# Attention with ternary gate on one core: maxima shared out by VectorE's time, masked keys computed one quad earlier, value transposes placed behind the next product, two groups of loads moved

## What is computed

```python
xn = layernorm(x)                                  # 1e-5
q, k, v = (xn @ W).reshape(B, T, 16, 32)           # for Wq, Wk, Wv
scores = einsum('bthd,bshd->bhts', q, k) * tril(ones((T, T)))
attn = softmax(scores / T ** 0.5)                  # masked keys keep score 0, not -inf
s = einsum('bhts,bshd->bthd', attn, v).reshape(B, T, 512) @ Wo
gate = silu(layernorm(xn, gamma, beta) @ ternary(weight).T + bias)
out = x + s * gate
```

## Time and profile before

| | |
|---|---|
| runs | 1616.06, 1619.94, 1622.37 us; median 1619.94 |
| profiled execution | 1617.84 us, span 1616.1 us, mean granted TensorE clock 0.972 |
| TensorE busy | 1524.8 us, 94% of the span |
| VectorE, ScalarE, GpSimd busy | 1052.3, 775.7, 868.5 us |
| phase A, its end, attention, phase D (us of the span) | 0 to 387, 387 to 420, 420 to 1490, 1490 to 1616 |

### The profile page before, as it was taken

How to read it: one execution, slowest core, us unless ns; L and a number is a source line. 1 busy time by engine, 2 the same in 40 slices (tenths; PEclk the granted TensorE clock), 3 DMA queues, 4 the chain that set the end, 5 groups by cost and what they waited for, 6 DMA issues and landing times.

```text
span 1616.1 us, 24521 instructions
## 1 busy us (share of the span) xinstructions
PE 1524.8 (94%) x8554; PEld 907.5 (56%) x8554; DVE 1052.3 (65%) x2389; ACT 775.7 (48%) x1614; POOL 868.5 (54%) x723
## 2 busy tenths in 40 slices
PE   6999999998799999999999999999999999899886
PEld 5777877786444455455544544544544554343665
DVE  7544765643687767767767776777766777650656
ACT  4333322233345565655656555665565655466110
POOL 4100000000565777877768777777776877469341
PEclk9999999999799999999999999999999999899999
DMA  6658765546931350351154146045025311211998
GB/s 202 188 179 216 237 196 183 157 157 181 215 90 34 80 145 21 82 113 56 35 114 116 35 86 145 15 98 132 23 53 119 92 35 38 89 32 55 305 343 294
DMA packets 110426, 201.42 MB, mean 125 GB/s; under 512 B 14688, under 2 KB 32736, under 8 KB 109280
## 3 DMA queue, kind: packets, MB, share of 16 engines
q1 hardware_dynamic: 99216, 177.86, 40.7%
q10 hardware_dynamic: 11088, 22.02, 4.1%
HBM read 123.22 MB, written 76.28 MB: 123 GB/s over the span
## 4 chain that ended last, share of the span: by engine, by line
PE 76%; DMA 9%; DVE 9%; SPq 2%; issue 1%; ACT 1%; POOL 1%; ACTq 0%; POOLq 0%; DVEq 0%
PE psP L1246 19%; PE psS L1316 17%; PE psO L1339 15%; PE psM L1224 14%; PE psL L1345 6%; DMA half<-mrow 3%; DMA gr<-gate 3%; DVE psM L1038 3%; DVE mx L1041 2%; PE psL L1354 2%; PE psT L1171 2%; DMA half<-k_lo 1%; SPq L546 1%; DMA rb<-r_rows 1%; ACT Pb L904 1%
## 5 line engine op out<-in xcount | busy, mean ns | idle before, releaser
L784 POOL TENSOR_TENSOR acc<-acc,Pb 128x1024 f32<-128x1024 f32 (+2 forms) x308 | 598.0, 1971 | 181.9 <-PE psO L1339 142.1
L904 ACT ACTIVATE Pb<-psS 128x512 f32<-128x512 f32 (+2 forms) x1122 | 519.6, 533 | 331.9 <-PE psS L1316 330.0
L1041 DVE TENSOR_REDUCE mx<-psM 128x1 f32<-128x512 f32 x768 | 485.8, 683 | 206.1 <-PE psM L1224 205.9
L1316 PE MATMUL psS<-half 97*128 97x512 f32 (+1 forms) x1247 | 476.9, 398 | 12.0 <-ACT Pb L904 7.4
L1224 PE MATMUL psM<-half 96*128 96x512 f32 (+3 forms) x1280 | 459.8, 387 | 29.0 <-DMA half<-k_lo 10.4
L1316 PEld LDWEIGHTS psS<-half 97*128 97x128 f32 x1247 | 235.9, 191 | 257.2 <-ACT Pb L904 99.1
L1224 PEld LDWEIGHTS psM<-half 96*128 96x128 f32 x1280 | 236.4, 192 | 108.0 <-DVE mx L1041 41.7
L1339 PE MATMUL psO<-Pb,Vs 128*32 128x512 f32 (+3 forms) x2304 | 272.5, 543 | 1.9 <-POOL Pb L767 1.9
L1038 DVE CUSTOM_DVE_ANT_0 psM<-psM,negm 128x256 f32<-128x256 f32 (+3 forms) x512 | 236.8, 518 | 51.5 <-PE psM L1224 50.7
L767 POOL TENSOR_SCALAR_AFFINE_SELECT Pb<-Pb 128x256 f32<-128x256 f32 x240 | 93.3, 405 | 112.5 <-ACT Pb L904 112.3
L727 POOL TENSOR_TENSOR rstd<-ve,mhalf 128x4 f32<-128x4 f32 x8 | 8.1, 1009 | 250.5 <-DVE ve L974 250.4
(11 more groups left out here) (101 smaller groups left out, 1472.7 us busy)
## 6 DMA issues: line engine op xcount, KB each, us to landing
half<-q_hi SPq DMA_DIRECT2D x32, 512.0 KB, 13.3
half<-k_hi SPq DMA_DIRECT2D x32, 512.0 KB, 11.2
xt<-in_L_attn_x SPq DMA_DIRECT2D x8, 1024.0 KB, 7.3
q_hi<-st_hi SPq DMA_DIRECT2D x32, 256.0 KB, 3.6
q_lo<-st_lo SPq DMA_DIRECT2D x32, 256.0 KB, 3.5
gate<-gs SPq DMA_DIRECT2D x32, 256.0 KB, 2.2
k_hi<-st_hi SPq DMA_DIRECT2D x32, 256.0 KB, 2.6
k_lo<-st_lo SPq DMA_DIRECT2D x32, 256.0 KB, 2.9
```

The source lines that it names most:

```text
L784: g.tensor_tensor(to[:, :, o:], to[:, :, o:], Pb[s % RING][:, heads, o:], ALU.add).then_inc(sum_done, 1)
L904: a.activation(weights(s, h)[:, o:], score_bank(s * HQ + h, last)[:, o:], ACT.Exp, scale=SCALE).then_inc(exp_done, 1)
L1041: ins = v.tensor_reduce(flat[:, heads, slots], bank[:, 0:ns * w].rearrange("p (a b c) -> p a b c", a=nh, c=w), AX.X, ALU.max)
L1316: t.matmul(score_bank(n, last)[:, o:], Ks[par][j // HALF][0:MROW + 1, h, j % HALF * P:(j % HALF + 1) * P], Qs[par][c // 2][0:MROW + 1, h, ...
```

## The change

1. **Plan.** `step_time` is replaced by a room per step (`step_room`), and shares are filled by cost (`COSTS`: 0.7 for a whole bank, 0.15 + 0.47 w / 512 per diagonal segment, 0.4 for a turn) and no longer by count. `UPFRONT` is now computed from both.
2. **Masked keys.** Those of chunk 0 of quad q+1 are made at group 16 of quad q (steps 32 and 33) on ScalarE and GpSimd; those of quad 0 stay at its start, and chunks 1 to 3 stay where they were.
3. **Phase A.** The value transposes of chunk n come behind the first query product of chunk n+1; VectorE's running sums (`sums`) move behind `low(0)` of chunk n+1. The last chunk's stay at the end. Query products now wait explicitly for `xl_done` of their chunk.
4. **First loads.** In the last chunk `load_half(0, 0, 1)`, `load_ones(0, 1)`, `load_chunk(0, 0)` and `load_values(0, 0)` are issued ahead of the key stores.
5. **Last weights.** In the last quad VectorE's reciprocals and split of Wo move from chunk 1 to chunk 3; SyncE's `reciprocals(0)` and `spread(0, 0)` move behind `store_chunk(7, 2)`.

```diff
--- before.py
+++ after.py
@@ -112,12 +112,36 @@
 TURN_LAG = 4
 
 
-def step_time(s):
-    return width(s) + P
-OWN = NMB * sum(step_time(s) for s in range(OWN_STEPS)) // sum(step_time(s) for s in range(NSTEP))
-UPFRONT = NMB - OWN
+def step_room(s):
+    c, j = STEPS[s]
+    ahead = STEPS[(s + 2) % NSTEP]
+    scores = 1.1 + 4.4 * (CW - max(0, ahead[1] - CT * ahead[0]) * P) / CW
+    section = 1.5 * width(s) / CW
+    return scores / 2.5 + section - (1 if j == 0 else 0)
+def bank_cost(bank):
+    segs = bank[0]
+    if diagonal(segs[0]):
+        return sum(0.15 + 0.47 * w / CW for _, _, _, w in segs)
+    return 0.7
+COSTS = [bank_cost(bank) for bank in MAXB]
+ROOM = [step_room(s) for s in range(NSTEP)]
+UPFRONT = min(k for k in range(NMB) if sum(COSTS[k:]) * sum(ROOM) <= sum(COSTS) * sum(ROOM[:OWN_STEPS]))
+def masked_keys(qn, gr):
+    found = [(qn, c) for c in range(NCH) if gr == FIRST[c] + (c > 0) and (c or qn == 0)]
+    if gr == FIRST[NCH - 1] + 4 and qn + 1 < NQUAD:
+        found.append((qn + 1, 0))
+    return found
 
 
 def max_order(banks):
@@ -150,10 +174,16 @@
         if z == len(pieces) - 1:
             first, end = first, first + 2
         steps = [(s, h) for s in range(first, end) for h in range(HQ)]
-        whole, past, k = sum(step_time(s) for s, _ in steps), 0, start
+        costs = [COSTS[e[2]] if e[0] == "bank" else 0.4 for e in order[start:upto]]
+        whole, cost, past, spent, k = sum(ROOM[s] for s, _ in steps), sum(costs), 0, 0, start
         for s, h in steps:
-            past += step_time(s)
-            to = start + (upto - start) * past // whole
+            past += ROOM[s]
+            to = k
+            while to < upto and (spent + costs[to - start] / 2) * whole < cost * past:
+                spent += costs[to - start]
+                to += 1
+            if (s, h) == steps[-1]:
+                to = upto
             shares[qn, s, h] = range(len(early) + k, len(early) + to)
             k = to
         start = upto
@@ -581,6 +611,13 @@
                 for j in range(CT):
                     sp.wait_ge(gs_done, START + n * CT + j + 1)
                     sp.dma_start(gate_t[n * CT + j], gs[j % 2][:]).then_inc(gs_out[j % 2], 16)
+                if n == NCHUNK - 1:
+                    sp.wait_ge(P_full, START + n * NPU + AT_GATE + CT)
+                    load_half(0, 0, 1)
+                    load_ones(0, 1)
+                    load_chunk(0, 0)
+                    load_values(0, 0)
                 for k in range(NQ, 2 * NQ):
                     store_parts(k)
                 if n == EARLY_CHUNKS[0] - 1:
@@ -594,13 +631,7 @@
                 if n == NCHUNK - 3:
                     store_maxima(0, 0)
                 if n == NCHUNK - 1:
                     store_maxima(0, 1)
-                    sp.wait_ge(P_full, START + n * NPU + AT_GATE + CT)
-                    load_chunk(0, 0)
-                    load_values(0, 0)
-                    load_half(0, 0, 1)
-                    load_ones(0, 1)
                     load_chunk(0, 1)
                 sp.wait_ge(vs_done, (n + 1) * CT)
                 for m in range(NQ):
@@ -661,7 +692,6 @@
                 store_maxima(qn, 2)
                 load_chunk(qn, 2)
                 if not more:
-                    reciprocals(0)
                     for i in range(2):
                         sp.wait_ge(ost_out[i], START + NQ * NCH // 2 * 16)
                         sp.dma_start(ac[i][:], numerators(0, i)).then_inc(ac_in[i], 16)
@@ -670,13 +700,13 @@
                 load_chunk(qn, 3)
                 if more:
                     store_maxima(qn + 1, 0)
-                else:
-                    spread(0, 0)
                 store_chunk(qn, 2)
                 if more:
                     load_chunk(qn + 1, 0)
                     store_maxima(qn + 1, 1)
                 else:
+                    reciprocals(0)
+                    spread(0, 0)
                     sp.wait_ge(wo_done, 2)
                     spread(0, 1)
                 if qn + 2 < NQUAD:
@@ -783,6 +813,18 @@
                             pool.wait_ge(sum_done, START + (qn * NG + summed_before(gr, not more)) * NPAIR + p - 1)
                         g.tensor_tensor(to[:, :, o:], to[:, :, o:], Pb[s % RING][:, heads, o:], ALU.add).then_inc(sum_done, 1)
 
+                def later_keys(qn, c):
+                    i, k = c % 2, qn * NCH + c
+                    pool.wait_ge(NE_done, START + k).then_inc(pool_waited, 1)
+                    g.iota(later[:], pattern=[[-1, CW]], base=T - 1 - c * CW, channel_multiplier=0,
+                           allow_small_or_imprecise_dtypes=True).then_inc(later_done, 1)
+                    pool.wait_ge(sub_done, START + k + 1)
+                    pool.wait_ge(E_done, START + k + 1)
+                    g.tensor_tensor(cum[i][:], cum[i][:], E[i][:], ALU.mult).then_inc(SE_done, 1)
+                    pool.wait_ge(SE_done, START + k + 1)
+                    pool.wait_ge(later_done, START + k + 1)
+                    g.tensor_tensor(E[i][:], later[:], E[i][:], ALU.mult).then_inc(NE_done, 1)
                 for gr, (c, j) in enumerate(GROUPS):
                     s = 2 * gr
                     if on_diagonal(s):
@@ -794,17 +836,8 @@
                             add(gr)
                     else:
                         add(gr)
-                    if gr == FIRST[c] + (c > 0):
-                        i, k = c % 2, qn * NCH + c
-                        pool.wait_ge(NE_done, START + k).then_inc(pool_waited, 1)
-                        g.iota(later[:], pattern=[[-1, CW]], base=T - 1 - c * CW, channel_multiplier=0,
-                               allow_small_or_imprecise_dtypes=True).then_inc(later_done, 1)
-                        pool.wait_ge(sub_done, START + k + 1)
-                        pool.wait_ge(E_done, START + k + 1)
-                        g.tensor_tensor(cum[i][:], cum[i][:], E[i][:], ALU.mult).then_inc(SE_done, 1)
-                        pool.wait_ge(SE_done, START + k + 1)
-                        pool.wait_ge(later_done, START + k + 1)
-                        g.tensor_tensor(E[i][:], later[:], E[i][:], ALU.mult).then_inc(NE_done, 1)
+                    for masked in masked_keys(qn, gr):
+                        later_keys(*masked)
 
             quads(quad)
 
@@ -907,17 +940,20 @@
 
             exps(0, 0)
 
+            def exp_masked(qn, c):
+                i = c % 2
+                act.wait_ge(e_in[i], (qn * (NCH // 2) + c // 2 + 1) * HQ * 16)
+                a.activation(E[i][:], E[i][:], ACT.Exp, scale=SCALE).then_inc(E_done, 1)
+                act.wait_ge(cum_in[i], (qn * (NCH // 2) + c // 2 + 1) * 16)
+                if c == 0:
+                    act.wait_ge(tot_in, (qn + 1) * 16)
+                a.activation(cum[i][:], cum[i][:], ACT.Identity, bias=tot[:, 0:1], scale=-1.0).then_inc(sub_done, 1)
             def quad(qn, par, more, follows):
                 for gr, (c, j) in enumerate(GROUPS):
                     exps(qn, 2 * gr + 1, not more)
-                    if gr == FIRST[c] + (c > 0):
-                        i = c % 2
-                        act.wait_ge(e_in[i], (qn * (NCH // 2) + c // 2 + 1) * HQ * 16)
-                        a.activation(E[i][:], E[i][:], ACT.Exp, scale=SCALE).then_inc(E_done, 1)
-                        act.wait_ge(cum_in[i], (qn * (NCH // 2) + c // 2 + 1) * 16)
-                        if c == 0:
-                            act.wait_ge(tot_in, (qn + 1) * 16)
-                        a.activation(cum[i][:], cum[i][:], ACT.Identity, bias=tot[:, 0:1], scale=-1.0).then_inc(sub_done, 1)
+                    for masked in masked_keys(qn, gr):
+                        exp_masked(*masked)
                     if gr + 1 < NG:
                         exps(qn, 2 * gr + 2, not more)
                     elif more:
@@ -1062,6 +1098,8 @@
                 if ahead:
                     moments(n + 1)
                 low(0)
+                if n:
+                    sums(n - 1)
                 low(1)
                 if ahead:
                     normal(n + 1)
@@ -1086,6 +1124,9 @@
                     if ahead:
                         x_low(n + 1, k)
                         y_low(n + 1, k)
+            def sums(n):
+                c = n % NCH
                 for m in range(NQ):
                     dve.wait_ge(V_full, START + n * NQ + m + 1)
                     dve.wait_ge(cs_out[m], START + n * 16)
@@ -1097,6 +1138,7 @@
                     v.tensor_copy(carry[:, m:m + 1], cs[m][:, CW - 1:CW]).then_inc(carry_done, 1)
 
             chunks(chunk)
+            sums(NCHUNK - 1)
 
             def reciprocals(b):
                 dve.wait_ge(lr_in, (b + 1) * 16)
@@ -1123,7 +1165,7 @@
                             maxima(max_share(qn, s, h))
                     if j == 0 and (c > 0 or follows):
                         denominators(*((qn, c - 1) if c else (qn - 1, NCH - 1)))
-                        if c == 1 and not more:
```

(9 more changed lines are left out.)

## The result

| | before | after |
|---|---|---|
| runs | 1616.06, 1619.94, 1622.17, 1622.37 us; median 1621.06 | 1576.30, 1576.94, 1579.03, 1580.55 us; median 1577.99 |
| ratio of the medians, 95% interval | | 0.9741 [0.9715, 0.9767] |
| profiled execution | 1617.84 us, span 1616.1, clock 0.972 | 1579.03 us, span 1577.3, clock 0.984 |

A forecast was written before the change was run, and what follows sets the result against it. TensorE's instruction order was taken to set the pace. Terms 5 + 12.4 + 10.7 + 16.1 = 44.2 us off the profiled 1617.84 gave 1573.6, kept as 1574 us; own range 1565 to 1582, 8 in 10 range 1559 to 1592.

The forecast's parts named there:

- Term 1: Phase A chunk boundaries: value transposes behind the next product remove seven 0.68 us waits; 5 us, between -2 and +6.
- Term 2: End of phase A: earlier first loads save TensorE's 10.36 us wait plus 2 for the clock; 12.4 us, ends 8 and 15.
- I take 2: Restart after phase A's load wait: full clock instead of half level gains between 1 and 3 us, taken as 2.
- rival (c): A moved load comes late, spreads or half loads: 10 to 15 us less, 1586 us; chance 11%.
- Term 3: Quad 7: moving reciprocals and Wo split from chunk 1 to chunk 3 removes the stall; 10.7 us, ends 7 and 12.
- Terms 4, 5 and the clock: Quad starts: masked keys 1.3, maxima plan 0.6, clock 0.4 us a quad; 16.1 us over seven quads.
- rival (b): Clock holds at quad starts, plan and keys give upper bounds: 57 us gained, 1561 us; chance 14%.
- Rival (a): Quad starts stay as they are, maxima-row or VectorE waits taking back the gain: 28 us remain, 1590 us; chance 20%.
- One of the prediction's own signs of being wrong: Quads: the prediction is wrong if the wait for the maxima rows grows beyond 1 us a quad.
- Rival (d): Group 16: ScalarE blocks in order on the next quad's masked-key loads; slower, 1742 us; chance 3%.
- Rival (e): Whole kernel: the change does nothing, half loads no earlier and other waits re-labelled; 4 us or less, 1614 us; chance 4%.

The follow-up runs named there:

- e10: Changed kernel with quad 1's second half of loads issued later in quad 0 and the first loads put back behind the key stores; median 1576.02 us, ratio 0.9716.
- e9: Changed kernel with quad 1's upper halves, ones and values issued behind chunk 2's maxima rows and masked-key loads, in quad 0 alone; median 1566.92 us, ratio 0.9676.
- e3: Changed kernel with only the first loads put back behind the key stores; median 1582.15 us, ratio 0.9763.
- e1: Changed kernel run again with no edit, as base for the others; median 1576.38 us, ratio 0.9730 to the kernel before.
- e6: Changed kernel with only the plan of the maxima put back; median 1597.71 us, ratio 0.9869.
- e4: Changed kernel with only reciprocals, Wo split and spreads put back; median 1584.05 us, ratio 0.9781.
- e8: Changed kernel with reciprocals and Wo split moved behind the last maxima of quad 7; median 1578.12 us, ratio 0.9749.
- e5: Changed kernel with only the masked keys put back to the quad's start; median 1595.64 us, ratio 0.9859.
- e11: Changed kernel with the next quad's upper half and values issued behind chunk 2's maxima rows and masked-key loads in quads 0 to 6; median 1565.00 us, ratio 0.9654.
- e12: e11 and e8 together: every quad's loads later, and reciprocals and Wo split behind quad 7's last maxima; median 1558.51 us, ratio 0.9635.
- e7: Changed kernel with masked keys and plan both put back; median 1602.63 us, ratio 0.9896.

## Why the prediction was right, and where it was not

| term | predicted | undone | by the profiles |
|---|---|---|---|
| 1 values turned | 5 | 6.1 | 7 x 0.89 = 6.2 |
| 2 first loads | 12.4 | 5.8 (9.1 in e10 against e9) | 9.3 (e3) or 10.1 (e10) gained, about as much lost in quad 0 |
| 3 last weights | 10.7 | 7.7 | 9.7 - 1.3 = 8.4 |
| 4, 5 and the clock | 7 x 2.3 = 16.1 | 26.3 | 3.4 a quad |
| sum | 44.2 | 45.9 | |

The four undone parts add up to 45.9 us, and the change gives 44.4 in e1's rounds (1620.82 - 1576.38). So within the scatter the parts add up, but for masked keys and plan. The predicted 44.2 met it because 6.6 and 3.0 too much in terms 2 and 3 stood against 10.2 and 1.1 too little in the others.

**Term 1** was right in mechanism, and in size by luck in part: the waits give the forecast's 4.8 us, and each boundary gave 0.2 more, which brings the term to 6.2, just above its upper end of 6. Another 1.7 us of phase A's gain in the first profile are chance (e1).

**Term 2** was too large already at the start of quad 0, and most of it was then lost. TensorE did keep the 10.36 us of the wait: undoing the move brings back 9.3 us there in e3 and 10.1 in e10. The "I take 2" for the clock did not come. The half level was not avoided; it moved from behind the stall to 392.7 to 402.5, behind the thin stretch at the end of phase A. The first two profiles seem to show 12.1 us at this place (20.2 less phase A's 8.1), but there the new plan helps too, with fewer maxima in steps 0 and 1: without it (e6) the same stretch takes 13.3 us instead of 11.9.

What the prediction missed is the next step on the same queue. "TensorE therefore keeps the 10.36 us" looked at the queue work that the moved loads pass, and not at that which follows them. TensorE starts quad 0 some 9 us sooner and SyncE asks for the maxima rows of chunk 2 10.1 us sooner (441.78 in e3, 431.71 now), but quad 1's loads ahead of them, 14 half and ones loads and the values, go out only 4.2 us sooner (411.81 and 407.65). The rows still have to wait for these, so in quad 0 the queue sets the pace. It is the shape of rival (c), a moved load that has another one come late. Shown by e9 and e10, which remove the wait by order alone and find 9 to 11 us for this term.

**Term 3** failed in "so the same 8 us of VectorE lie beside nothing." No maxima were beside it, but GpSimd's adds were, and both became slower: 12.46 against 9.41 us for four adds, 7.12 against 3.54 for cast and subtraction. GpSimd had no idle time left there, so ScalarE and then TensorE stood behind it. The stall of 7.49 us and what came after it in chunk 1 was sized about right (9.7 us between e4 and e1, 11.2 between the first two profiles), and the spreads kept their cover. The two engines had met in the kernel before as well: in chunk 1 the cast took 2.03 us and the subtraction 4.31, against 1.17 and 2.37 alone.

The Trainium skill, "SBUF — State Buffer", section "🔬 SBUF: two separate sides", says that VectorE and GpSimd share one pair of ports as an exclusive lock, held for a whole instruction, when VectorE's instruction runs in a two-port mode or, against a GpSimd instruction that reads SBUF, has two SBUF inputs. The trace agrees as far as it goes: by that rule GpSimd would be held for at most the cast's and the subtraction's own 1.17 + 2.37 = 3.54 us (an estimate, from e8's durations), and it lost 12.46 - 9.41 = 3.05. The single instructions end in turn, each about its own time alone behind the one before: the second add at 1414.46, the cast (alone 1.17 us) at 1415.55, the third add (alone 2.35) at 1417.80, the subtraction (alone 2.37) at 1419.96, the fourth add at 1422.19. That the cast runs in a two-port mode is not shown. The rule would have spoken against "beside nothing".

**Terms 4, 5 and the clock** were right in direction and wrong in how they are put together. The split 1.3 for the keys, 0.6 for the plan and 0.4 for the clock supposed that they add. They do not: alone each gives 0 to 0.2 us a quad (e5, e6). The measured 3.4 a quad are 13.6 / 6 = 2.3 of clock and 1.1 of the rest. From a quad's last values to the next one's first, 6.1 us became 4.8, a gain of 1.3; the later wait for maxima rows grew by 1.0; the remaining 0.8 lies in later steps, and no row here places it. So the part without clock was near the 1.9 forecast less what the DMA took, and the clock was mis-sized: 0.4 against 2.3. The forecast took a fall at half its price and at a chance of a half. The fall came at none of the seven starts, in this profile and in seven of nine others with both parts, and before it had cost more than 1.7 us where it was twice as long (6.8 us, as at 700.7). It is no certainty either: in e11 and e12 the clock fell at two and at three starts. That the wait for the maxima rows would take some of it back was right in place, and in size 1.0 us a quad.

This is rival (b)'s mechanism, the clock holds, at a price of 3.4 a quad against its 4.2, together with shortfalls in terms 2 and 3. Rival (a) fell, since the wait for maxima rows grew but did not take back the whole. One of the prediction's own signs of being wrong did appear: this wait is 8.0 us over six quads, 1.3 a quad and so beyond its 1 us, and 17.5 us with quad 0's 9.5. The sum held in spite of it. Rival (d) fell: ScalarE had no idle time ahead of the masked keys at all (groups by line; busy, mean ns, idle before; the exponential's line shows 0.0 too):

```profile
L950 ACT ACTIVATE cum<-cum,tot 128x512 f32<-128x512 f32 x32 | 23.4, 732 | 0.0
```

Rival (e) fell in all parts.

What is not settled: why exactly the clock falls at one start and not at another, and so whether the denser starts are what gave the 2.3 us. Over the profiles the two go together: with 4.5 to 5.3 of 5.90 us busy ahead of the first values (before, e5 to e7) it fell at 25 of 28 starts, and with 5.38 in the changed kernel and in e1 to e4 and e8 to e10 at none of 56. But with 5.38 or more ahead it fell at 5 of 14 in e11 and e12, and no run varied only the work ahead of a start.

## What to carry to other kernels

When a transfer on a queue is moved ahead, follow the queue past it: what comes next on it starts earlier too, and a small transfer that an engine needs soon may then stand behind megabytes that nobody needs yet; put these behind the small one. Two engines that end together ahead of a third must be relieved together, and the test of one edit alone can say that it is worth next to nothing. Where work is moved "beside nothing", look at what the other engines do at that time, and not only at the one that it runs on. A gain read from two profiles of different kernels can belong to several edits and to chance; undo one edit, and compare the same stretch.

## What the runs showed of the hardware

- The clock fell behind light stretches with no long idle time. At the quad starts of the kernel before TensorE was busy 4.8 to 5.0 of 5.90 us, and 3.4 or 6.8 us at the 1.2 GHz level followed or began there, at all seven starts. In the changed kernel, with 5.38 of 5.90 us, it fell at none, and the difference, 13.6 us in six quads, is two thirds of what the two edits gave there. It is a tendency and not a rule: it stayed at a start with 4.86 (e6, quad 6) and fell at one with 5.38 (e11, quad 5).
- An add of GpSimd (128x1024, both inputs in SBUF) takes 2.35 us in a row alone. Beside VectorE's cast and subtraction of 128x2048 two adds take 3.40 and 4.42 us, while the cast goes from 1.17 to 2.75 us and the subtraction from 2.37 to 4.37. Neither shows a wait: the busy time grows.
- On one DMA queue four small transfers of maxima rows issued at 431.71, behind 7.4 MB of halves and values of the next quad issued from 407.65 to 419.3, were used at 445.16, 13.5 us after their issue. Behind the same loads, begun 30 us and not 24 us ahead of them (e3), they were used after 7.0 us, and with half of these loads put behind them (e9) after 3.9.
